# Even and odd nodes: a 17-tap convolution by three half-length sums, and a new order of the slot

## What is computed

```python
x = _layernorm(x + L0(x, adj));  x = _layernorm(x + L1(x, adj))
x = _layernorm(x + L2(x, adj));  x = _layernorm(x + L3(x, adj, nodemask))

# L0: two convolutions along the nodes, distances, messages, a gated cell
h = relu(bn1(conv1d(xc, conv1_w, 0)))
h = bn2(conv1d(h, conv2_w, 8))                 # 17 taps, 128 -> 128 features
x_conv = relu(h + xc).T
s = x @ w_se.T + b_se;  A = exp(-dist(s)) * mask
x_nmp = A @ relu(x @ w_msg.T + b_msg)
gi = concat(x_conv, x_nmp) @ w_ih.T + b_ih;  gh = x @ w_hh.T + b_hh
r = sigmoid(gi_r + gh_r);  z = sigmoid(gi_z + gh_z);  n = tanh(gi_n + r * gh_n)
return (1 - z) * n + z * x
# L1: A = adj * sigmoid(leaky(x W_q) leaky(x W_k)^T / sqrt(128)), degree-normalised, times leaky(x W_lin + b)
# L2: adj @ logmap0(x), then expmap0 and project (norms, artanh, tanh per node)
# L3: relu(mask * (normalised (adj + I)) @ (x W^T + b))
```

## Time and profile before

| | before |
|---|---|
| median of three runs | 819.48 us |
| profiled execution: time, span | 819.74 us, 817.6 us |
| PE busy | 754.8 us (92%) |
| DVE busy | 575.5 us (70%) |
| ACT busy | 436.9 us (53%) |
| POOL busy | 145.8 us (18%) |
| one steady slot | 47.40 us |
| HBM traffic | 92 GB/s mean |

### The profile page before, as it was taken

How to read it: one execution, slowest core, us unless ns; L and a number is a source line. 1 busy time by engine, 2 the same in 40 slices (tenths; PEclk the granted TensorE clock), 3 DMA queues, 4 the chain that set the end, 5 groups by cost and what they waited for, 6 DMA issues and landing times.

```text
span 817.6 us, 11746 instructions
## 1 busy us (share of the span) xinstructions
PE 754.8 (92%) x3552; PEld 538.8 (66%) x3552; DVE 575.5 (70%) x1945; ACT 436.9 (53%) x941; POOL 145.8 (18%) x166
## 2 busy tenths in 40 slices
PE   5999999999999999999999999999999999998743
PEld 3667767676776767677676767777676777756531
DVE  6255778676777867677786867687686768775666
ACT  4363827457283746728374663838466372833441
POOL 0000122122111212212121221212121111221221
PEclk9999999999999999999999999999999999998886
DMA  5333330423333032333304133330413233011000
GB/s 193 116 116 104 104 116 13 128 92 118 114 105 126 13 134 84 128 103 115 116 18 145 68 128 103 115 116 28 149 54 128 103 115 116 2 52 65 1 13 26
DMA packets 46582, 75.29 MB, mean 92 GB/s; under 512 B 4064, under 2 KB 12768, under 8 KB 46432
## 3 DMA queue, kind: packets, MB, share of 16 engines
q1 hardware_dynamic: 46560, 75.02, 27.4%
HBM read 70.82 MB, written 4.19 MB: 92 GB/s over the span
## 4 chain that ended last, share of the span: by engine, by line
PE 70%; ACT 19%; issue 5%; DVE 4%; POOL 1%; DMA 0%; ACTq 0%; SPq 0%; POOLq 0%; DVEq 0%
PE K L1177 13%; PE CONV L1208 12%; PE F L1295 7%; PE K L1322 7%; PE C L1288 6%; PE C L1217 5%; PE F L1217 5%; ACT X L392 5%; ACT A L430 4%; PE F L1145 2%; PE F L1196 2%; PE F L1277 2%; PE K L1170 2%; PE K L1310 2%; PE K L1275 2%
## 5 line engine op out<-in xcount | busy, mean ns | idle before, releaser
L1208 PE MATMUL CONV<-H1H,WH 128*128 128x512 f32 x272 | 119.1, 438 | 6.4 <-DVE H1L L692 6.3
L1208 PE MATMUL CONV<-H1L,WH 128*128 128x512 f32 x272 | 107.6, 396 | 0.0
L1208 PE MATMUL CONV<-H1H,WL 128*128 128x512 f32 x272 | 107.4, 395 | 0.0
L312 POOL TENSOR_TENSOR RSTD<-VEPS,POW 128x4 f32<-128x4 f32 x48 | 50.1, 1044 | 271.1 <-DVE VEPS L674 271.1
L1208 PEld LDWEIGHTS CONV<-H1H,WH 128*128 128x128 f32 x272 | 51.6, 190 | 26.6 <-issue 16.3
L495 ACT ACTIVATE G<-K 128x512 f32<-128x512 f32 x16 | 9.6, 597 | 108.5 <-PE K L1322 108.4
L1288 PE MATMUL C<-QT,KT 128*128 128x512 f32 x128 | 59.9, 607 | 0.7 <-ACT BIG L435 0.7
L1208 PEld LDWEIGHTS CONV<-H1L,WH 128*128 128x128 f32 x272 | 51.7, 190 | 12.7 <-issue 3.8
L1208 PEld LDWEIGHTS CONV<-H1H,WL 128*128 128x128 f32 x272 | 51.5, 189 | 12.0
L1177 PE MATMUL K<-XS,BIG 128*128 128x128 f32 x496 | 58.0, 275 | 0.0
L1295 PE MATMUL F<-A,MSG 128*128 128x512 f32 x128 | 57.5, 592 | 0.0
(11 more groups left out here) (236 smaller groups left out, 1740.4 us busy)
## 6 DMA issues: line engine op xcount, KB each, us to landing
ADJF<-in_adjT SPq DMA_DIRECT2D x16, 1024.0 KB, 5.3
ADJN<-in_adj SPq DMA_DIRECT2D x16, 1024.0 KB, 5.2
ADJM<-in_adjT SPq DMA_DIRECT2D x15, 1024.0 KB, 5.2
ADJR<-in_adjT SPq DMA_DIRECT2D x14, 1024.0 KB, 5.2
X_IN<-in_xT SPq DMA_DIRECT2D x16, 256.0 KB, 2.5
out<-OUT SPq DMA_DIRECT2D x16, 256.0 KB, 2.3
BIG<-in_weights SPq DMA_DIRECT2D x1, 1088.0 KB, 5.6
BIG<-in_weights SPq DMA_DIRECT2D x1, 576.0 KB, 8.6
```

What stands on the lines that cost most here:

```text
L312: nc.gpsimd.tensor_tensor(RSTD[:, row, :], VEPS[:, row, :], POW[:, 0, :], ALU.pow).then_inc(ev[f"ln{layer}_rstd"], 1)
L1208: last = mm(CONV[:, :], w[:, W_CONV2 + k * P:W_CONV2 + (k + 1) * P], h[:, k:k + N], start=(k == 0 and i == 0), stop=(k == TAPS - 1 and i = ...
```

## The change

The nodes are permuted on the host, the even ones first and then the odd ones, in x, in both axes of adj and in the mask; the output's store puts them back. With the node halves e and o and the taps split into 9 even ones (w0, w2, ...) and 8 odd ones (w1, w3, ...), the kernel forms three products instead of four: the odd taps on the sum of the two halves (HS), a set of weight differences on the even nodes and another on the odd nodes. The sum's product goes into K0 and counts for both halves (`conv_part`). The differences are formed on VectorE at the start, in the tile ADJN. The padding of a half is 4 columns on either side.

```diff
+PH = N // 2
+EDGE = HALF // 2
+PADDED = PH + 2 * EDGE
-            V.memset(H1H[:, :].bitcast(F32), 0.0)
+            V.memset(H1H[:, :, :].bitcast(F32), 0.0)
+            V.memset(H1[:, :, :], 0.0)
+            def sum_of_h1(count, previous):
+                dve.wait_ge(ev["h1_ready"], count)
+                V.tensor_tensor(HS[:, 0:PADDED - 1], H1[:, 1, 0:PADDED - 1], H1[:, 0, 1:PADDED], ALU.add).then_inc(
+                    ev["hs_ready"], 1)
+                dve.wait_ge(ev["hs_ready"], count)
+                dve.wait_ge(ev["conv2_done"], previous)
+                V.tensor_copy(HSH[:, 0:PADDED - 1], HS[:, 0:PADDED - 1]).then_inc(ev["hsh_ready"], 1)
+                dve.wait_ge(ev["hsh_ready"], count)
+                V.tensor_tensor(HSL[:, 0:PADDED - 1], HS[:, 0:PADDED - 1], HSH[:, 0:PADDED - 1].bitcast(F32),
+                                ALU.subtract).then_inc(ev["hsl_ready"], 1)
             rest_of_x(1, 0)
             dve.wait_ge(s_conv2_w, 16)
-            split(W_CONV2, W_IH, 2)
+            V.tensor_tensor(less_even, even[:, P:EVEN * P], odd, ALU.subtract)
+            V.tensor_tensor(less_odd, even[:, 0:ODD * P], odd, ALU.subtract).then_inc(s_leading, 1)
+            split(S_EVEN, even[:, 0:P], 3)
+            split(S_EVEN + P, less_even, 4).then_inc(s_split, 1)
             rest_of_h1(1, 0)
             stacked(1)
+            split(S_ODD, less_odd, 5)
+            split(S_ODD + ODD * P, even[:, ODD * P:EVEN * P], 6).then_inc(s_split, 1)
+            split(S_SUM, odd, 7).then_inc(s_split, 1)
+            sum_of_h1(1, 0)
             dve.wait_ge(s_plain_w, 48)
             V.tensor_tensor(WF[:, P:5 * P], WF[:, P:5 * P], W[:, W_SPLIT:W_SPLIT + 4 * P], ALU.subtract).then_inc(
                 s_less, 1)
-            def gated(n):
-                V.tensor_tensor(NG[:, :], NG[:, :], XT[:, :], ALU.subtract).then_inc(ev["gate_d"], 1)
...
+            def gated(count):
+                dve.wait_ge(ev["n_ready"], count)
                 V.tensor_tensor(NG[:, :], NG[:, :], WG[:, :], ALU.mult).then_inc(ev["gate_e"], 1)
...
+                V.tensor_tensor(Y[:, :], NG[:, :], XT[:, :], ALU.subtract).then_inc(ev["y_ready"], 1)
+            def kept_state(count):
+                dve.wait_ge(ev["w_ready"], count)
+                V.scalar_tensor_tensor(XT[:, :], WG[:, :], -2.0, XT[:, :], ALU.add, ALU.mult).then_inc(ev["gate_x"], 1)
+            def conv_part(n):
+                dve.wait_ge(ev["conv2_sum"], n["f"])
+                dve.wait_ge(ev["xcopy"], n["f"])
+                V.scalar_tensor_tensor(phased(XC), twice(K0[:, 0:PH]), SC[:, 1:2], phased(XT), ALU.mult,
+                                       ALU.add).then_inc(ev["xconv_part"], 1)
+            def taps(at_col, a, b, out, high, low, count):
                 for k in range(a, b):
-                        last = mm(CONV[:, :], w[:, W_CONV2 + k * P:W_CONV2 + (k + 1) * P], h[:, k:k + N],
+                        last = mm(out, w[:, at_col + k * P:at_col + (k + 1) * P], h[:, k:k + PH],
+            def even_taps(a, b):
+                return taps(S_EVEN, a, b, CONV[:, 0:PH], H1H[:, 0, :], H1L[:, 0, :], EVEN)
+            def odd_taps(a, b):
+                return taps(S_ODD, a, b, CONV[:, PH:N], H1H[:, 1, :], H1L[:, 1, :], EVEN)
+            def sum_taps(n):
+                pe.wait_ge(ev["hsl_ready"], n["f"])
+                pe.wait_ge(ev["str_ready"], n["f"])
+                pe.wait_ge(ev["x_raw"], n["m"])
+                taps(S_SUM, 0, ODD, K0[:, 0:PH], HSH[:, :], HSL[:, :], ODD).then_inc(ev["conv2_sum"], 1)
-                product(F1[:, :], [(weight(W_SE), (XH[:, :], XL[:, :]))]).then_inc(ev["g1_done"], 1)
+                product(K0[:, :], [(weight(W_SE), (XH[:, :], XL[:, :]))]).then_inc(ev["g1_done"], 1)
```

The factors, their squares, `parts` and `stacked` use K0 in place of F1. The order of TensorE's steps in a slot becomes (steps that only some slots have stand without their condition):

```diff
@@ TensorE body
-first_taps (2), distances01, taps(2, 4), state_by_nodes, distances23, messages, taps(4, 9),
-first_norm_by_features, support, projections, taps(9, 12), attention, summed_messages, taps(12, 14),
-own_gates, taps(14, 16), last_aggregation, attention_degree, taps(16, 17), reset_gate_of_x,
-gates_of_messages, last_linear, attended, reset_gate_of_conv, first_conv, factors, update_gate,
-own_squares, new_gate
+distances01, state_by_nodes, distances23, messages, even_taps(0, 8), first_norm_by_features,
+even_taps(8, 9), odd_taps(0, 2), projections, odd_taps(2, 8), attention, support, sum_taps,
+odd_taps(8, 9), summed_messages, own_gates, attention_degree, reset_gate_of_x, last_aggregation,
+gates_of_messages, last_linear, reset_gate_of_conv, factors, first_conv, update_gate, own_squares,
+new_gate, attended
```

VectorE applies the first norm (from K0) in place of ScalarE, and takes the attended sum of the graph before (`first_residual`) between the first norm's statistics and its application:

```diff
@@ VectorE body
-tangent_norm, gated, artanh_ratio, first_norm_stats, artanh_series, tangent, masked0, message_sum,
-leaky, leaky_linear, degree_guard, own_loops, ball_factor, second_residual, attention01, scaled_norm,
-attention23, third_norm, degree_mask, rest_of_messages, attention_degree, conv_residual,
-scaled_attention, rest_of_conv, rest_of_x, last_residual, reset, first_residual, rest_of_h1,
-new_input, stacked
+first_norm_stats, first_residual, first_norm, second_norm_moments, message_sum, sum_of_h1,
+tangent_norm, artanh_ratio, artanh_series, leaky, leaky_linear, degree_guard, tangent, attention01,
+masked0, attention23, own_loops, conv_part, ball_factor, second_residual, rest_of_messages,
+scaled_norm, third_norm, degree_mask, conv_residual, attention_degree, scaled_attention,
+rest_of_conv, rest_of_x, last_residual, reset, rest_of_h1, new_input, stacked, kept_state, gated
@@ ScalarE body
-new_state, exps(0, 2), second_norm, artanh_log, exps(2, 4), keep_x, first_norm,
-first_norm_by_features, messages, degrees, queries_and_keys, support_norms, linear, sigmoids(0, 2),
-support_tanh, sigmoids(2, 4), output, summed_messages, last_sums, convolved, leading_x, reset_gate,
-squares, first_conv, parts, update_gate
+new_state, exps(0, 4), keep_x, degrees, first_norm_by_features, messages, queries_and_keys,
+second_norm, artanh_log, linear, sigmoids(0, 4), support_norms, support_tanh, output,
+summed_messages, convolved, last_sums, leading_x, reset_gate, squares, first_conv, update_gate, parts
@@ GpSimd body
-rstd(0), shift(0), degree_power, norm_power, rstd(2), attention_power, rstd(3), shift(3),
-second_norm_powers
+rstd(0), second_norm_powers, degree_power, norm_power, rstd(2), attention_power, rstd(3), shift(3)
```

More of the change, by code:

```diff
@@ L521, in body @@
                 act.wait_ge(ev["agg0_done"], n["f_prev"])
-                exps(n, 0, 2)
+                exps(n, 0, C)
+                keep_x(n)
+                if rear:
+                    degrees(n)
+                if mid:
+                    first_norm_by_features(n)
+                messages(n)
+                if mid:
+                    queries_and_keys(n)
                 if rear:
@@ L1024, in body @@
                 if rear:
+                    first_residual(n, n["r"], n["r_prev"])
+                if mid:
+                    first_norm(n)
+                if rear:
+                    second_norm_moments(n["r"])
+                message_sum(n)
+                if not n["first"]:
+                    sum_of_h1(n["f"], n["f_prev"])
+                if rear:
+                    tangent_norm(n)
+                    artanh_ratio(n)
                     artanh_series(n)
-                    tangent(n)
-                masked0(n)
-                message_sum(n)
                 if mid:
@@ L1229, in first_taps @@
                     pe.wait_ge(s_split, 2)
-                taps(0, 2)
+                even_taps(0, 8)
             def distances01(n):
@@ L1315, in reset_gate_of_x @@
                 pe.wait_ge(ev["nmph_ready"], n["f"])
-                gate(F1, True, False, [(weight(W_HH), xt)]).then_inc(ev["x_used"], 1)
+                gate(F1, True, False, [(weight(S_HH), xt)]).then_inc(ev["x_used"], 1)
             def last_aggregation(n):
@@ L1400, in body @@
                 new_gate(n)
+                if mid:
+                    attended(n)
             def ending():
                 a, b, c = counts(pe, B - 1), counts(pe, B), counts(pe, B + 1)
-                first_taps(a)
                 distances01(a)
-                taps(2, 4)
                 state_by_nodes(a)
```

304 lines of the change are left out of this document (157 added, 147 removed).

## The result

| | before | after |
|---|---|---|
| median of the runs shown beside each other | 819.70 us | 798.43 us |
| ratio, with its 95% interval | | 0.9732 [0.9718, 0.9746] |
| span of the profiled execution | 817.6 us | 796.2 us |
| own squares to own squares, mean of the 13 slots behind slot 1 | 47.43 us | 45.28 us |
| own squares of slot 0, of slot 1, at | 41.05, 81.48 us | 45.48, 83.89 us |

The change makes the kernel 2.7% faster. The forecast was 788 in a range of 770 to 808; the time came out 10 us above the forecast, inside the range. The gain between the spans is 21.4 us where 31.3 were worked out.

The account below looks back on a forecast made before the run. TensorE was taken as the bound, with 45.4 of 47.4 us per slot matmul work without a gap. First two slots -0.7, thirteen slots 13 x -2.4 = -31.2, end +0.6: 819.5 - 31.3 = 788 us, range 770 to 808.

Parts of the forecast that it names:

- Rival 2: Slots: chain shorter than walked, matmul work alone bounds; 43.4 to 44.2 us per slot, 765 to 778 us; chance 0.13.
- Rival 3: Conv taps: weight load sets a half-length matmul's pace; at 0.19 us each, slower, 849 us; chance 0.07.
- Rival 1: More chain exposed than walked, or lower clock in slot 0; slot 45.9 to 47, 800 to 814 us; chance 0.25.
- VectorE's row of thirteen operations: Steady slot, attention halves, masks, own loops and conv part: VectorE runs without a break, 8.3 us to 28.8.
- the one from the tanh to the first norm: Steady slot: state's transposes at 4.85 without a gap, norm done at 10.6, TensorE there at 10.05, waiting about 0.6 us.
- At FS the walk: Steady slot, before the last sums: FS ready at 34.9, TensorE there at 33.9, a new wait of about 1.0 us.
- XX's wait: Steady slot: VectorE idle before XX, behind ScalarE's linear copy, from 16.6 to 18.4, some 1.8 us.
- The idle before the messages: Slot 0: TensorE's messages wait for VectorE's flag, an idle of 3.5 us that ends the slot 3.5 later.
- distances start without a gap: Steady slot: the attended sum covers the wait, distances start at 4.27 us; the earlier gap of 0.34 goes.
- The last slot and the drain keep their chain: End: attended sum sliding in +1.3 us, state's first step done early -0.7, together +0.6.
- the conv work (-2.0): Each slot's taps: 78 matmuls at 0.126 us take 9.8 us, 2.0 less than before.
- the gaps (three that go, one for FS that comes): TensorE per slot: waits before taps (0.62), distances (0.34), state's transposes (0.25) go; about 1.0 us before last sums comes.

Follow-up runs that it names:

- linear_first: Changed kernel with ScalarE's linear copy moved ahead of the second norm, logarithm and table load: 795.25 us, 0.9685 of the kernel before.
- linear_taps: linear_first with eleven taps instead of eight ahead of the first norm's transposes, three odd ones behind them: 794.53 us, 0.9687 of the kernel before.
- norm_act: Changed kernel with the first norm given back to ScalarE, ahead of the degrees: 817.33 us, 0.9956 of the kernel before.
- quarter: Changed kernel with each tap streaming only 128 of a half's 256 columns, same number of matmuls and loads: 821.94 us, one execution.
- tail: Changed kernel with reset gate of x and gates of the messages ahead of the last sums in the last slot: 794.29 us, 0.9686 of the kernel before.
- order_only: Kernel before with only the new order of all engines, convolution still 17 taps on 512 nodes: 824.14 us, ratio 1.0046.
- half_only: Kernel before with only the half-length convolution, in the old order: 827.24 us, ratio 1.0085.
- attended_back: Changed kernel with TensorE's attended sum back in its old place, ahead of the convolution's reset gate: 860.37 us, 1.0491 of the kernel before.
- start: Changed kernel with VectorE's difference of the plain weights ahead of the splits of odd and summed taps: 794.56 us, 0.9679 of the kernel before.

## Why the prediction was right or wrong

**Bound and direction: right.** That a chain through VectorE and ScalarE holds the slot, and takes back part of the saved matmul work, is what `linear_first`, `linear_taps`, `norm_act` and the page's chain show. Rival 2 (matmul work alone) is out: `quarter` took matmul work away and the slot at full clock went from 45.30 to 45.23. Rival 3 is out: the step is 0.119, although the loads last 0.19. Rival 1 came in part: its low clock and its idle at the start did, its slots of 45.9 and more did not, and 798 lies just below its 800. VectorE's row of thirteen operations ran without a break, as walked (467.57 to 475.8, 8.2 us for 8.3).

**The price of a half-length matmul: mis-sized.** 0.126 was taken, 0.1185 measured. The 0.019 us by which float32r was dearer than float32 was read as a fixed amount per matmul; nearly all of it goes by the column. 78 x 0.0075 = 0.6 us a slot were in TensorE's favour, and as `quarter` shows such a gift stays with the waits.

**The slot: 45.0 forecast, 45.28 measured.** Counted from the end of the own squares (446.85), the distances started at 4.2 as walked. The step that failed is the one from the tanh to the first norm: Y was ready 0.15 late and its transposes waited 0.36 (forecast: none), the statistics began 0.45 late, and the norm ended 0.3 late; TensorE was there 0.1 early, so its wait is 1.05 for 0.6. The attention took 0.25 more than its matmuls, for which the walk had no wait. At FS the walk was right to 0.1 (35.0 for 34.9); TensorE came to it 0.45 later than walked, hence 0.78 for 1.0. XX's wait was right, 2.05 for 1.8. By the gains per slot it is 13 x (2.40 - 2.16) = 3.1 us.

**The first two slots: +2.4 for -0.7.** Slot 0 was to end 3.5 later and ended 4.4 later, a difference within the spread of 1.9 us between equal slots 0; slot 1 was to win 4.2 and won 2.0. The idle before the messages came as forecast (3.20 for 3.5). The steps that failed are "distances start without a gap", which was walked for a steady slot and carried to the first two, and the price of an idle, taken as its length: rival 1 had the low clock, at 2.5 us, outside the sum. In slot 1 TensorE ran at half rate from 49.32 to 56.2, less the 0.78 of idle; matmuls of 6.1 us at half rate are 3.1 us too long, an estimate from these rows which is more than the 2.2 missed.

**The end: +4.2 for +0.6.** "The last slot and the drain keep their chain" failed. In the hand-written last slot the last sums stand ahead of the gates of the messages, so there is nothing to cover FS; `tail` shows that with them ahead 3.1 us return. The remaining 1.1 lie in drain matmuls that are the same and take longer: the support's first sixteen 3.75 us for 3.40, the two sets of last sums 6.02 and 5.60 for 5.30 and 5.24, while the waits between them are the same to about 0.1. Others are quicker (the drain's first projection 1.44 for 2.08), so the half-rate stretches fall elsewhere; the mean granted clock of the last 70 us is 0.74, before 0.76. Why is open.

**What no step of it said:** the two parts of the change are worth nothing, or less, alone. The prediction priced the conv work (-2.0) and the gaps (three that go, one for FS that comes) as terms of a sum. The slots of `order_only` (-0.3) and `half_only` (-0.1) against both (-2.15) show that they are not: the saved work counts only where the order lets the chain keep up. The sum came out near the truth because the walk was made for both at once.

## What to carry to other kernels

Where one engine is at 97% of a steady stretch, as here, work taken from it can come back as waits unless the order of the other engines is tightened in the same change, so price both by one walk, and test them together before either is dropped. Look at the places where a pipeline has no neighbour yet or any more (the first boundary, the last slot): an order that covers a wait with the neighbour's work has no cover there. And count an idle of some 2 us on TensorE at more than its length: look at the granted clock of the stretch behind it.

## What the runs showed of the hardware that was not expected

- float32r matmuls of 128 rows: 0.233 us at 512 columns, 0.119 at 256, 0.111 at 128. At 128 the step is the cadence of the weight loads, 0.11, although a load is recorded with 0.19.
- Behind an idle of two to three microseconds TensorE ran at half rate for several more: 6.9 us in slot 1 of after (49.32 to 56.2), and in its slot 0, where a second idle of 3.20 followed, from 16.09 to 25.5. In a steady slot the same idle of 2.29 (`attended_back`) went with 2.1 us on top of its length.
- The granted clock doesn't show every such stretch. It reads 0.50 in 50.00 to 55.00 of after, but 1.00 in 20.00 to 22.00 of `start`, where the taps still start 0.21 apart. In these traces what it misses is the first stretch of the program, before TensorE first reaches full rate: up to 21.88 in `start`, up to 46.57 in `quarter`. The distances between starts of equal matmuls tell more.
- How soon full rate came differed even with equal matmuls: in slot 0 with taps of 256 columns at 25.45 in after and at 27.6 in `linear_first`. With taps of 128 columns it came not before 46.57.
